# A gated cross-attention block: a value projection split around a small product on TensorE

## The reference

```python
V = linear(ctx, Wv, bv)                      # per batch: 375 x 256, contraction over 256
qk = einsum('bhqd,bhkd->bhqk', Q, K)
feats = stack([mean_sim, max_sim, entropy_proxy])          # three numbers per batch and head
hidden = gelu(linear(feats, w1, b1))         # 64 wide
hidden = gelu(linear(hidden, w2, b2))
t = exp(clip(linear(hidden, w3, b3), LOG_T_MIN, LOG_T_MAX))
attn = softmax(qk / (2 t));  out = linear(attn @ V, Wo, bo)
x = x + tanh(g_xattn) * out
x = x + tanh(g_ffn) * ffn(layernorm(x))      # gate, up, down, with quantised operands
```

## Time and profile before

| | us |
|---|---|
| runs | 902.7, 904.37, 899.25; median 902.7 |
| profiled execution, its own time | 901.26 |
| its span (first to last instruction) | 899.5 |
| TensorE busy | 734.9 |
| VectorE busy | 724.4 |
| ScalarE busy | 706.6 |
| GpSimd busy | 503.8 |
| granted TensorE clock, mean | 0.949 of full |

### The profile page before, as it was taken

One profiled execution on the slowest core, in us unless ns is written; L12 is line 12 of the kernel. 1 busy time (PEld: TensorE's weight loads), 2 busy tenths in 40 slices (PEclk: granted clock), 3 DMA queues, 4 the chain that ended last, 5 costly groups with the idle time before them and its releaser, 6 DMA issues.

```text
span 899.5 us, 21270 instructions
## 1 busy us (share of the span) xinstructions
PE 734.9 (82%) x7309; PEld 490.8 (55%) x7322; DVE 724.4 (81%) x1501; ACT 706.6 (79%) x1445; POOL 503.8 (56%) x965
## 2 busy tenths in 40 slices
PE   2554788989898999899898999898888876686797
PEld 1332455656565666566565666565655555353454
DVE  1646887979898979898898979898988766597996
ACT  1146688888888888988888888889889786586896
POOL 6555857575655747575757565575633210364564
PEclk9975789999999989999999989999998899799999
DMA  9587445445454545564554645555530122121222
GB/s 242 137 234 167 112 98 119 110 110 121 117 133 113 137 113 132 118 138 117 130 115 114 132 100 138 109 140 117 150 86 22 42 75 81 40 70 59 77 78 77
DMA packets 119704, 101.64 MB, mean 113 GB/s; under 512 B 27359, under 2 KB 115999, under 8 KB 119583
## 3 DMA queue, kind: packets, MB, share of 16 engines
q1 hardware_dynamic: 119598, 100.28, 45.2%
HBM read 50.00 MB, written 12.85 MB: 70 GB/s over the span
## 4 chain that ended last, share of the span: by engine, by line
PE 37%; DVE 23%; ACT 23%; issue 7%; SPq 5%; DMA 2%; POOL 1%; DVEq 0%; ACTq 0%; POOLq 0%
PE p_m L1139 9%; ACT ex L960 7%; PE p_o L1069 7%; ACT pt L950 7%; PE p_m L1122 6%; DVE stats L724 6%; DVE nm L743 6%; PE p_s L1052 4%; ACT L967 2%; PE p_s L1203 2%; DVE kst L860 2%; DVE va L674 2%; DVE hmax L863 2%; PE p_t L1170 2%; SPq L379 2%
## 5 line engine op out<-in xcount | busy, mean ns | idle before, releaser
L724 DVE BATCH_NORM_STATS2 stats<-ex 112x6 f32<-112x375 f32 x512 | 253.7, 538 | 53.9 <-ACT ex L960 53.0
L960 ACT ACTIVATE ex<-p_s,nm 112x375 f32<-112x375 f32 x512 | 269.5, 594 | 12.6 <-DVE nm L743 12.6
L950 ACT ACTIVATE pt<-p_t,ct 128x336 f32<-128x336 f32 x488 | 239.5, 550 | 49.8 <-PE p_t L1170 48.4
L743 DVE TENSOR_REDUCE nm<-p_s 112x2 f32<-112x750 f32 x256 | 237.2, 926 | 12.6 <-PE p_s L1052 12.4
L1052 PE MATMUL p_s<-kst,qst 96*112 96x375 bf16 x512 | 135.5, 348 | 35.3 <-ACT ex L960 31.8
L1170 PE MATMUL p_t<-qst,kst 99*128 99x112 bf16 x1464 | 122.4, 215 | 10.7 <-ACT pt L950 7.1
L1170 PEld LDWEIGHTS p_t<-qst,kst 99*128 99x128 bf16 x1464 | 93.8, 99 | 59.5 <-ACT pt L950 23.0
L1139 PE MATMUL p_m<-ctxt,wk_sb 128*128 128x375 f32 x256 | 109.9, 555 | 16.5 <-DMA ctxt<-ctxt_dram 10.8
L1122 PE MATMUL p_m<-wv_sb,ctxt 128*128 128x256 f32 (+1 forms) x384 | 110.4, 412 | 5.0 <-DVE on L712 4.7
L1069 PE MATMUL p_o<-pt,va 128*32 128x112 f32 (+1 forms) x3072 | 104.6, 271 | 8.0 <-ACT pt L950 6.3
L1069 PEld LDWEIGHTS p_o<-pt,va 128*32 128x32 f32 (+1 forms) x3072 | 72.8, 113 | 45.7 <-issue 40.0
(11 more groups left out here) (162 smaller groups left out, 1225.8 us busy)
## 6 DMA issues: line engine op xcount, KB each, us to landing
kst<-kp SPq DMA_DIRECT2D x384, 93.8 KB, 3.4
ctxt<-ctxt_dram SPq DMA_DIRECT2D x32, 375.0 KB, 3.6
qbounce<-qp SPq DMA_DIRECT2D x32, 168.0 KB, 2.7
qst<-qbounce SPq DMA_DIRECT2D x32, 168.0 KB, 2.7
xa<-x_dram SPq DMA_DIRECT2D x32, 112.0 KB, 2.7
qst<-qbounce SPq DMA_DIRECT2D x32, 112.0 KB, 2.7
xm<-x_dram SPq DMA_DIRECT2D x32, 112.0 KB, 2.3
x_dram<-x SPq DMA_DIRECT2D x32, 112.0 KB, 2.1
```

The source lines that it names most:

```text
L724: last = nc.vector.bn_stats(stats[:, nb % RING, 2 * pb + i], ex[0:SQ, 2 * (t % 2) + i, :])
L743: nc.vector.tensor_reduce(nm[:, n % RING, 2 * p:2 * p + 2], p_s[t % 2][0:SQ, :, 0:SK], axis=AX.X, op=ALU.max, negate=True).then_inc(s_max, 1)
L950: nc.scalar.activation(pt[:, (2 * r + i) % 8], st_home(r, i)[:, 0:KC * SQ].rearrange("k (c q) -> k c q", c=KC), ACT.Exp, scale=ct[:, nr % ...
L960: last = nc.scalar.activation(ex[0:SQ, 2 * ((t - 1) % 2) + i, :], p_s[(t - 1) % 2][0:SQ, i, 0:SK], ACT.Exp, bias=nm[:, ne % RING, h:h + 1])
```

## The change

In a gelu slot the third value piece is taken apart at its two contraction halves. The wait for `on` and the product over the first half now stand ahead of the wait for the first gelu and of the second product; the product over the second half stays behind it and releases the reader as before. The partial sum stays open in `p_m` across the second product, which goes to another accumulator (`t_h2`, in `p_o`). All other slots issue the same instructions as before.

```diff
+                def values(ch, ks):
+
+                    for k in ks:
+                        last = mm(p_m[0:KEYS[ch], 0:D], ctxt[:, v % CRING, k, ch * KR:ch * KR + KEYS[ch]], wv[:, k, :], start=(k == 0), stop=(k == C - 1))
+                    return last
+
                 if p == 7 and pair_of(n):
+                    if active("V2", n):
+                        take("V2", n)
+                        values(2, (0,))
                     pe.wait_ge(s_g1, n // 2)
                     mm(t_h2, w2t[:, :], hid1[:, :], start=True, stop=True).then_inc(s_h2, 1)
...
                     ch = {1: 0, 2: 1, 7: 2}[p]
-                    take(f"V{ch}", n)
-                    if v == 0 and ch == 0:
-                        pe.wait_ge(s_w, 16 * WEIGHTS)
-                    for k in range(C):
-                        last = mm(p_m[0:KEYS[ch], 0:D], ctxt[:, v % CRING, k, ch * KR:ch * KR + KEYS[ch]], wv[:, k, :], start=(k == 0), stop=(k == C - 1))
-                    last.then_inc(s_vmm, 1)
+                    if p == 7 and pair_of(n):
+                        values(ch, (1,)).then_inc(s_vmm, 1)
+                    else:
+                        take(f"V{ch}", n)
+                        if v == 0 and ch == 0:
+                            pe.wait_ge(s_w, 16 * WEIGHTS)
+                        values(ch, range(C)).then_inc(s_vmm, 1)
```

## The result

| kernel | median us | runs | against before, 95% interval |
|---|---|---|---|
| before | 903.42 | 11 | |
| changed | 910.14 (907.76 to 913.71) | 11 | 1.0077 [1.0057, 1.0097] |

The changed kernel is 6.7 us slower.

What follows compares the result with a forecast made beforehand. ScalarE's own chain was taken to set the time in the gelu slot. Passes 0, slot at 690.9 0, last slot +0.9 and clock -1.4 gave -0.5 us on 902.7, so 902.2 us, range 897.0 to 907.5.

Steps and rivals of the forecast that it cites:

- Two passes ahead: 14 steady gelu slots: 0.56 us of value passes fit the 0.86 idle ahead of the second product; cost 0.
- two behind: Steady gelu slots: weighted values start 0.56 us earlier, but transposed scores still wait for `pt`; gain 0, at most 7.8 us.
- the slot at 690.9: Gelu slot before the last: passes end at about T-0.01 (T: first gelu's end), second product just met; cost 0 to 0.1, taken 0.
- Rival (c): Ahead of line 1104: two passes outlast 0.86 us and delay the second product; +8.7 us, 911.4, chance 0.07.
- The last slot: Last gelu slot: second product, behind `on` and two passes, 0.8 to 1.3 us late; ends 0 and +1.3, taken +0.9.
- The clock: TensorE's clock in the gelu slots: one fall to 1.2 GHz less, as falls follow the filled hole; -1.4 us.
- The bounds: Limits set for the clock term: -4.9 us if falls go, +10.8 if four dearer falls replace two.
- The sign by which the prediction wanted to be found wrong: Pair of batches without a clock fall: prediction wrong if its 41.34 us changes by more than 0.1 us.
- (d): Idle of 1.02 us after the weighted values brings four clock falls at 2.4 us; +6.8, 910.4 with last slot, chance 0.09.
- (a): All 16 gelu slots: TensorE's time counts after all, 9.0 us go, less 0.9; 894.6, chance 0.06.
- (b): All clock falls behind gelu slots go: -4.9 + 0.9 = -4.0 us, 898.7, chance 0.12.

Runs made afterwards that it cites:

- The whole piece ahead: Changed kernel with all four value passes, not two, ahead of the second product in 15 gelu slots, last gelu slot in the old order; 911.21 us, 1.0108 of before.
- the last slot as before: Changed kernel with the last gelu slot put back in the order of before, the other 15 keeping the split; 911.11 us, 1.0088 of before.
- only the last slot split: Kernel before with the split in the last gelu slot alone; 903.75 us, 1.0017 of before.
- the old idle filled: Kernel before with a throwaway copy of the first half product ahead of the second product in 15 gelu slots, value piece whole behind; 900.01 us, 0.9961 of before.

## Why the prediction was wrong

*Two passes ahead, cost 0; two behind, gain 0; the slot at 690.9, 0 to 0.1.* Right. The second gelu stands at T+0.39 to T+0.40 in all 14 steady slots and at T+0.46 in the one before the last, a pair without a fall is 41.34 us, and the new idle is for `pt`. The idle was forecast at 0.30 and 1.02 and came out at 0.43 and 0.89, since half of the 1.12 us is too much for two passes. That duration reaches past the start of what follows: from start to start the piece behind the second product took 1.06 us with four passes and takes 0.63 with two (281.26 to 281.89), so two passes moved 0.43 us. The whole piece ahead shows the same from the other side: four passes fitted into the idle of 0.86 and cost nothing. Rival (c) needed two passes longer than those 0.86 us, and no steady slot came near it.

*The last slot, +0.9.* The place was right (the gelu late by 1.1 us, forecast 0.8 to 1.3), the price isn't confirmed: three comparisons put it at -1.0 (changed, against the one with the last slot as before), +1.5 (1.0017) and +0.8 us, each within an interval of some 3 us either way.

*The clock, -1.4: here the prediction failed.* The step was "one fall less, as the falls follow the hole that is filled but the sum of idle stays". In the profiled execution this term was +7.8 in the steady stretch: two falls became six. Two errors made it. The sign: I took the idle ahead of the second product as what brings the falls and the idle behind as its harmless remainder; yet 0.89 or 1.07 us behind the weighted values bring five or six falls in twelve pairs, while 0.46 there, with the same 0.43 ahead, brings none. And the price: I took -1.4 from the falls at T+1.1, where 1.10 of 2.52 us lie under idle that is there for ScalarE's sake. From T+3.6 on ScalarE waits for TensorE, and 6.8 us at the lower clock cost 2.3 to 2.5 us. The bounds held, -4.9 to +10.8, and so did the warning in them that a later fall is dearer; the value taken inside them had no row behind it. The sign by which the prediction wanted to be found wrong, a changed pair without a fall, never came: it watched the slot, and the loss was in the clock.

*The rivals.* (d) is what happened, forecast at 910.4 for a measured 910.1, with a chance of 0.09; it named the mechanism, the place and, nearly, the price: four falls at 2.4 us were assumed, three at 2.3 to 2.5 and three cheaper ones were found. That the medians meet within 0.3 us is luck in part: 0.9 of the 910.4 is the unconfirmed term of the last slot, and the traces are 11.3 us apart, not 7.7. Its argument against, that the sum of idle is that of before, is what the runs refute: equal sums (0.86 + 0.46 and 0.43 + 0.89, with 0.60 ahead of both) gave 903.4 and 910.1. (a) is refuted by the pairs of 41.34. (b)'s hope was sound for the idle ahead alone: filling it without a new one gave -0.4%.

The Trainium skill, page "TensorE: Matmul & The Clock Gate", section "A second HAM failure mode: psum-queue depth-cycling", tells of a kernel in which short idles between groups of matmuls are enough to make the clock swing between its two levels. The traces here agree: no idle longer than 0.89 us stands in a steady gelu slot of the changed kernel and none longer than 1.07 in the one with the whole piece ahead, and the clock fell six and five times in twelve pairs.

*What stays open.* Why equal idle brings more falls behind the weighted values than ahead of the second product: the traces show that it does, not why. And where the tail's 3.9 us come from: the tail is 174.73 us with only the last slot as before and 174.78 with only the last slot split, but 170.72 with the old idle filled, so one trace each doesn't part the last slot's share from the falls'.

## What to carry to other kernels

Moving TensorE work from one side of a wait to the other moves the idle too; if the slot's end is set by another engine, nothing is gained, and here the clock was lost. Ask of every idle stretch of TensorE what comes after it: here the one in front of slots in which TensorE is waited for was the dear one. Where idle can't be avoided, repeated work whose result is thrown away, put exactly there, was worth 0.4% here and undid a loss of 0.8%; put elsewhere it cost 3% more than the changed kernel.

## What the hardware showed beside this

Fifteen times 24 additional passes two slots ahead of the gelu slot cost not some 9 us (an estimate: 24 passes took 0.58 us of the idle that they filled) but 30 against the changed kernel. In the trace the start of the fall moved from T+2.9 in the second of the twelve pairs to T+3.5 in the sixth, and from there the pairs stayed at 44.34 to 44.38 us with a fall at the same place every time: this kernel, with its steady period, stayed in a state in which every period has its fall. What would take it out again wasn't tried.
